# A selective-scan stage re-laid: 32 channels by 4 states per instruction, operands spread by DMA, decays in PSUM

## The chip, the cores and the metric

One core of one Trainium2 chip runs the whole program. The metric is device time in microseconds (us): the median of three runs, with one further execution taken by the profiler.

## What is computed

Two layers, each a Mamba block on a sequence of 2304 tokens (four images of 24 x 24, pixel-shuffled) and then a mixture of experts. The change touches only the Mamba block, cut here to what matters:

```
u = silu(conv4(in_proj(x)) + conv_b)             # 128 channels
dt, B, C = split(x_proj(u))                      # B and C: 16 states each
dt = softplus(dt_proj(dt) + dt_b)                # 128 channels
for each step:
    h[d, n] = exp(dt[d] * A[d, n]) * h[d, n] + dt[d] * u[d] * B[n]
    y[d]    = sum_n h[d, n] * C[n]
out = out_proj((y + u * D) * silu(z))
```

Everything is in float32. Softplus is computed as relu(x) + ln(1 + e) plus what the rounding of 1 + e lost, with e = exp(-|x|).

## The kernel before

`mamba` works through 24 tiles of T = 384 steps. Each engine has its own program, written out by hand, and the engines meet only at semaphores; each engine takes its instructions in the order written. An inner loop over n goes through the 16 states. Channels lie on the 128 partitions and one instruction takes one state, 128 x 384:

- ScalarE `decay` (L487) writes exp(dt * A[n]) into `da`, a ring of eight buffers in SBUF (`NDA` = 8), so it can be eight states ahead of the scan.
- TensorE `spread_b` (L373) spreads row n of B over all partitions by a bf16 matmul with a selector; B is held as a sum of three bf16 parts, which VectorE splits off (`split_one` L560, `split_two` L568) with two ScalarE copies.
- VectorE `times_b` (L577) multiplies w = dt * u with the spread B in place in PSUM, and `scan` (L586) runs the recurrence h = da * h + dbu along the 384 steps.
- GpSimd `times_c` (L657) multiplies h with C spread over the partitions. C gets there by DMA: its rows are stored (`c_rows`, L701) and read back by four broadcasting transfers (`crep`, L706).
- TensorE `sum_y` (L382) adds the 16 products up in PSUM by matmuls with the identity; `skip` (L378) starts the sum with u * D. The sum has two PSUM banks in turn.

For the next tiles, between those: TensorE `u_in` (L345), `z_in` (L355), `project_bc` (L362), `project_dt` (L366), and `project_out` (L388) for the tile before; ScalarE `silu_u` (L457), `silu_z` (L463) and six softplus steps (L226 to L244) with three table loads a tile (L536, L538, L542); GpSimd four additions and products that end softplus and form w (L248 to L262); VectorE `gate` (L593, y times silu(z)) and `residual` (L598, which adds `project_out`'s result to X). `project_out` and `z_in` share one PSUM bank, `zb_ps`: `z_in` of the next tile waits for `residual`.

## Time and profile before

| | |
|---|---|
| median of 3 runs | 2034.57 us (2032.19 to 2036.46) |
| the profiled execution | 2032.55 us, span of its instructions 2030.8 us |
| first to last scan, layer 0 | 46.96 to 622.3 us |
| VectorE busy | 1483.5 us (73% of the span) |
| TensorE matmul busy | 1643.1 us (81%) |
| GpSimd busy | 1216.9 us (60%) |
| ScalarE busy | 981.5 us (48%) |

Busy shares are means over stages with different limits. Two stretches of the span, one for each layer, are the Mamba blocks; the rest (norms, routing, experts, combining) is not touched. In a timeline row an instruction can start before the one ahead of it is over, so start-to-start distances are what adds up.

### The profile page before, as it was taken

Reading aid. Unit: us, or ns where it says so; the run is one execution under the profiler, and the core shown is the slowest. Engines: PE = TensorE matmul, PEld = TensorE weight load, DVE = VectorE, ACT = ScalarE, POOL = GpSimd, SP = SyncE. Lnnn points to the kernel's source line nnn. Section 1 sums busy time; section 2 is a strip of 40 time slices with the busy share of each in tenths; the row PEclk is TensorE's granted clock in tenths of the full one; section 3 lists DMA queues with packets and bytes.
Section 4 is the critical chain, followed back from the end, with each engine's and each line's share of the span. In section 5 each row is a group of like instructions: output and inputs, shape, how many; then the busy total and the mean of one; then the engine's idle time right before and its main releaser. Section 6 shows DMA issues by size and latency. Waiting matters only on the chain. (4 is left out here: it accounts for less than half of the span.)

```text
span 2030.8 us, 31247 instructions
## 1 busy us (share of the span) xinstructions
PE 1643.1 (81%) x7952; PEld 1124.3 (55%) x7953; DVE 1483.5 (73%) x2441; ACT 981.5 (48%) x1739; POOL 1216.9 (60%) x1409
## 2 busy tenths in 40 slices
PE   6888888888878399999946888888888874699994
PEld 4444444444435299999934444444444433599992
DVE  4999999999995522222246999999999986444443
ACT  6777677766763011111137777667766643011111
POOL 1888888888882135454305888888888860355440
PEclk8999999999999699999977999999999997799996
DMA  4344433333336301011033334433333326011114
GB/s 157 128 141 142 143 134 125 125 125 125 125 125 259 135 32 38 34 39 34 29 118 125 126 134 141 144 143 126 125 125 125 125 82 276 27 52 46 46 44 148
DMA packets 60049, 227.06 MB, mean 112 GB/s; under 512 B 8448, under 2 KB 23680, under 8 KB 56576
## 3 DMA queue, kind: packets, MB, share of 16 engines
q1 hardware_dynamic: 51744, 203.93, 28.1%
q0 software_dynamic: 8256, 22.56, 3.4%
q8 instruction: 21, 0.34, 0.1%
q14 instruction: 28, 0.23, 0.0%
HBM read 206.92 MB, written 19.53 MB: 112 GB/s over the span
## 5 line engine op out<-in xcount | busy, mean ns | idle before, releaser
L657 POOL TENSOR_TENSOR L_hc<-L_h,L_crep 128x384 f32<-128x384 f32 x768 | 775.2, 1018 | 211.1 <-DVE L_h L586 211.1
L382 PE MATMUL ps<-L_hc,ident 128*128 128x384 f32 x1536 | 622.4, 487 | 0.9 <-POOL L_hc L657 0.8
L577 DVE TENSOR_TENSOR ps<-L_w,ps 128x384 f32<-128x384 f32 x768 | 414.9, 540 | 20.4 <-PE ps L373 10.4
L487 ACT ACTIVATE L_da<-L_dt,L_negA 128x384 f32<-128x384 f32 x768 | 414.9, 604 | 15.6 <-DVE L_h L586 15.0
L373 PE MATMUL ps<-L_parts,sel 96*128 96x384 bf16 x768 | 256.3, 335 | 183.6 <-DVE L_h L586 177.3
L586 DVE TENSOR_TENSOR_SCAN L_h<-L_da,L_carry,ps 128x384 f32<-128x384 f32 x384 | 384.6, 1002 | 0.0
L586 DVE TENSOR_TENSOR_SCAN L_h<-L_da,L_h,ps 128x384 f32<-128x384 f32 x384 | 383.6, 999 | 0.0
L373 PEld LDWEIGHTS ps<-L_parts,sel 96*128 96x128 bf16 x768 | 73.4, 96 | 501.7 <-DVE L_h L586 494.3
L382 PEld LDWEIGHTS ps<-L_hc,ident 128*128 128x128 f32 x1536 | 270.9, 193 | 39.4 <-issue 6.2
L1114 DVE COPY Xn<-L_w 128x2048 f32 x86 | 107.8, 1256 | 117.6 <-PE ps L1064 108.8
L1097 ACT ACTIVATE L0e_hT<-ps 128x512 f32<-128x512 f32 x86 | 51.4, 597 | 267.4 <-PE ps L1064 267.4
L1064 PE MATMUL ps<-L0e_xT,Xn 128*128 128x128 f32 x1376 | 159.7, 277 | 2.8 <-DVE Xn L1114 2.8
L1064 PEld LDWEIGHTS ps<-L0e_xT,Xn 128*128 128x128 f32 x1376 | 159.4, 194 | 4.3 <-issue 3.2
L1064 PE MATMUL ps<-L1e_xT,Xn 128*128 128x128 f32 x1376 | 158.9, 277 | 2.6 <-DVE Xn L1114 2.6
L1064 PEld LDWEIGHTS ps<-L1e_xT,Xn 128*128 128x128 f32 x1376 | 158.2, 194 | 4.5 <-issue 2.9
L1079 PE MATMUL ps<-L_w,L0e_hT 128*128 x688 | 152.2, 379 | 0.9 <-ACT L0e_hT L1097 0.9
L1079 PEld LDWEIGHTS ps<-L_w,L0e_hT 128*128 128x128 f32 x688 | 129.0, 190 | 17.7 <-issue 1.1
L1097 ACT ACTIVATE L1e_gl<-ps 128x512 f32<-128x512 f32 x43 | 25.7, 598 | 217.6 <-PE ps L1064 217.6
L345 PEld LDWEIGHTS ps<-Xn,L_fold 128*128 128x128 f32 x480 | 89.5, 199 | 38.8 <-ACT L_sp_r L229 3.5
L345 PE MATMUL ps<-Xn,L_fold 128*128 (+1 forms) x480 | 105.4, 338 | 2.3 <-ACT L_sp_r L229 2.3
L1002 POOL TENSOR_TENSOR L0e_give_done<-ones 128x1 f32<-128x1 f32 x44 | 8.5, 194 | 164.0 <-DVE L0e_yt L1136 162.2
L1136 DVE COPY L0e_yt<-ps 128x512 f32<-128x512 f32 (+1 forms) x22 | 14.9, 680 | 123.2 <-PE ps L1079 123.2
(270 smaller groups left out, 2052.0 us busy)
## 6 DMA issues: line engine op xcount, KB each, us to landing
L_crep<-c_rows SPq DMA_DIRECT2D x192, 768.0 KB, 7.6
L_w<-in_up SPq DMA_DIRECT2D x16, 1024.0 KB, 11.9
L_w<-in_down SPq DMA_DIRECT2D x8, 1024.0 KB, 26.9
tok_rows<-Xn SPq DMA_DIRECT2D x6, 768.0 KB, 13.1
L0s_got<-results SPq DMA_DIRECT2D x18, 256.0 KB, 2.8
L1s_got<-results SPq DMA_DIRECT2D x18, 256.0 KB, 3.3
L_w<-in_down SPq DMA_DIRECT2D x8, 512.0 KB, 21.3
X<-in_x SPq DMA_DIRECT2D x4, 576.0 KB, 7.7
```

What stands on the lines that cost most here:

```text
L345: mm = nc.tensor.matmul(ua_ps[:, j * (T // 2):(j + 1) * (T // 2)], fold[:, g, :], column(t, img, back), start=(k in (0, 2)), stop=(k in (1 ...
L373: nc.tensor.matmul(b_ps(n), m["sel"][:, n, :], parts[0:BC, r, :], start=True, stop=True).then_inc(sem["b"], 1)
L382: nc.tensor.matmul(y_ps[r], ident[:], hc[:, n % NHC, :], start=False, stop=(n == N - 1)).then_inc(sem["y"], 1)
L487: nc.scalar.activation(da[:, n % NDA, :], dt[:, r, :], ACT.Exp, scale=negA[:, 0, n:n + 1]).then_inc(sem["da"], 1)
L577: nc.vector.tensor_tensor(b_ps(n), w[:, r, :], b_ps(n), ALU.mult).then_inc(sem["dbu"], 1)
L586: nc.vector.tensor_tensor_scan(h[:, n, :], da[:, n % NDA, :], b_ps(n), first, ALU.mult, ALU.add).then_inc(sem["scan"], 1)
L657: nc.gpsimd.tensor_tensor(hc[:, n % NHC, :], h[:, n, :], crep[:, r, n, :], ALU.mult).then_inc(sem["hc"], 1)
L1064: mm = nc.tensor.matmul(ps[:, h * NBH + b, (f % BF) * TS:(f % BF + 1) * TS], w1_t[:, h, i, f * P:(f + 1) * P], xT[:, r, i, h, :], start=(i ...
L1079: mm = nc.tensor.matmul(ps[:, 7, h * D:(h + 1) * D], hT[:, r, h, f, :], w2[:, bass.ds(e[h], 1), f, :].rearrange("p e d -> p (e d)"), start ...
L1097: nc.scalar.activation(dst, ps[:, h * NBH + b, :], ACT.Silu if gated else ACT.Gelu).then_inc(sem["act"], 1)
L1114: nc.vector.tensor_copy(w1_t[:, h].rearrange("p i f -> p (i f)"), w1[:, bass.ds(e, 1)].rearrange("p e i f -> p (e i f)")).then_inc(sem["st ...
L1136: nc.vector.tensor_copy(yt[:, r, 0:n, :].rearrange("p h d -> p (h d)"), ps[:, 7, 0:n * D]).then_inc(sem["yev"], 1)
```

## The change

The state is laid out otherwise. Partition 32 n + d now holds channel d of a group of 32 channels and the n-th quarter of the states, so one instruction takes 32 channels x 4 states; column c = 4 k + g is state k of each quarter and channel group g. There are still 16 columns of 128 x 384 a tile.

- dt and w must now stand in every quarter. TensorE adds the three parts of softplus in PSUM (`add_relu`, `add_log`), of which GpSimd forms only the lost rounding (`lost`); ScalarE copies dt out (`take_dt`), VectorE forms w (`times_u`). SP stores both (`dw_rows`, 384 KB) and reads them back into `dwq` by four transfers of 384 KB, one for each quarter of the partitions, and then C and the last four states' B from `cb_rows` into `cbq` by four of 240 KB. In place of that, the spread of C to 128 partitions goes (3 MB a tile).
- B of 12 states is spread by three float32 matmuls a tile; the three-part bf16 split goes. One instruction multiplies two columns: six a tile on VectorE, into SBUF, two on GpSimd (`times_b`).
- Decays are written to PSUM, three banks in turn (`DA_RING` = 3) in place of eight buffers in SBUF.
- `times_c` takes two columns at a time (eight a tile in place of sixteen).
- `sum_y` takes four columns at a time: four float32 matmuls with a 128 x 32 matrix, each into its own 32 partitions of the sum. The sum has one PSUM bank; `skip` waits for the gate of the tile before.
- ScalarE computes Ln with the table set that has Exp too, so two table loads a tile are left. Softplus of tile t + 2 is worked on in tile t.

```diff
-NDA, NHC = 8, 8
-NBP = 4
-LEAD, LAG = 3, 5
-A0, A1 = 4, 11
-D_GATE, D_SPLIT, D_RES = 5, 2, 8
-P0, P1 = 5, 7
-CN = 4
+Q = 4
+QW = P // Q
+QR = Q + 1
+DA_RING = 3
...
+        def da(r, c):
+            return bank((r * N + c) % DA_RING)
+        def b_ps(r, k):
+            return bank(3 + (r + k) % 2)
+        y_ps, ua_ps, zb_ps = bank(5), bank(6), bank(7)
...
             def u_in(t, img, which):
                 if 0 in which:
-                    wait(pe, sem["relu"], t)
+                    wait(pe, sem["w"], t)
+                    wait(pe, sem["dt_out"], t)
...
+            def add_relu(t):
+                pe.wait_ge(sem["relu"], t + 1)
+                nc.tensor.matmul(ua_ps, ident[:], sp["r"][:], start=True, stop=False)
+            def add_log(t):
+                pe.wait_ge(sem["l"], t + 1)
+                nc.tensor.matmul(ua_ps, ident[:], sp["l"][:], start=False, stop=False)
+                pe.wait_ge(sem["lost"], t + 1)
+                nc.tensor.matmul(ua_ps, ident[:], sp["a"][:], start=False, stop=True).then_inc(sem["dt"], 1)
+            def spread_b(t, r, k):
+                wait(pe, sem["dbu"], 6 * t + 2 * k - 2)
+                nc.tensor.matmul(b_ps(r, k), w_b[:, k, :], u[:, r, :], start=True, stop=True).then_inc(sem["b"], 1)
             def skip(t, r):
-                wait(pe, sem["yz"], t - 1)
-                nc.tensor.matmul(y_ps[r], diagD[:], u[:, r, :], start=True, stop=False)
-            def sum_y(t, r, n):
-                pe.wait_ge(sem["hc"], t * N + n + 1)
-                nc.tensor.matmul(y_ps[r], ident[:], hc[:, n % NHC, :], start=False, stop=(n == N - 1)
-                                 ).then_inc(sem["y"], 1)
+                wait(pe, sem["yz"], t)
+                nc.tensor.matmul(y_ps, diagD[:], u[:, r, :], start=True, stop=False)
+            def sum_y(t, r, k):
+                pe.wait_ge(sem["hc"], 8 * t + 2 * k + 2)
+                for g in range(Q):
+                    mm = nc.tensor.matmul(y_ps[g * QW:(g + 1) * QW, :], same[:, 0:QW], hc[:, (k % 2) * Q + g, :],
+                                          start=False, stop=(k == Q - 1))
+                mm.then_inc(sem["y"], 1)
...
+                if more:
+                    add_relu(t + 1)
+                    add_log(t + 1)
+                if not first:
+                    sum_y(t - 1, 1 - r, Q - 1)
+                spread_b(t, r, 2)
+                if more == 2:
+                    u_in(t + 2, img2, (0, 1))
+                if not first:
                     if more:
-                        if n == 0:
-                            project_bc(t + 1, 1 - r)
-                        if n == 1:
-                            project_dt(t + 1, 1 - r)
-                    if more == 2 and 4 <= n <= 6:
-                        u_in(t + 2, img2, ((0, 1), (2, 3), (4,))[n - 4])
-                    if n == 6 and not first:
-                        if more:
-                            pe.wait_ge(sem["r1"], t + 2)
-                        project_out(t - 1)
-                    if n == 8 and more:
-                        z_in(t + 1, img1)
+                        pe.wait_ge(sem["bc_out"], t + 2)
+                    else:
+                        pe.wait_ge(sem["zs"], t + 1)
+                    project_out(t - 1)
+                skip(t, r)
+                if more == 2:
+                    u_in(t + 2, img2, (2, 3, 4))
+                sum_y(t, r, 0)
+                if more:
+                    spread_b(t + 1, 1 - r, 0)
+                    wait(pe, sem["bc_out"], t + 2)
+                    wait(pe, sem["res"], t)
+                    z_in(t + 1, img1)
+                sum_y(t, r, 1)
+                if more:
+                    spread_b(t + 1, 1 - r, 1)
+                if more == 2:
+                    project_dt(t + 2, r)
+                    pe.wait_ge(sem["zs"], t + 2)
+                    project_bc(t + 2, r)
+                sum_y(t, r, 2)
...
+            def take_dt(t, before):
+                act.wait_ge(sem["dt"], t + 1)
+                for s, count in before:
+                    wait(act, s, count)
+                nc.scalar.activation(dw[:, 0, :], ua_ps, ACT.Identity, bias=ln_one[:, 1:2]).then_inc(sem["dt_out"], 1)
...
+            def decay(t, r, p, c):
+                at = r * N + c
+                if c == 0:
+                    act.wait_ge(s_dw[r], 64 * (p + 1))
+                if at < DA_RING:
+                    wait(act, sem["scan"], 2 * N * p + (-1, 0, -2)[at])
+                else:
+                    act.wait_ge(sem["scan"], 2 * N * p + at - DA_RING + 1)
+                nc.scalar.activation(da(r, c), dwq[:, r, c % Q, 0, :], ACT.Exp, scale=negA[:, 0, c:c + 1]
                                      ).then_inc(sem["da"], 1)
...
+            def tile(t, r, p, more):
+                for c in range(N):
+                    decay(t, r, p, c)
+                    if c == 1 and more:
+                        take_dt(t + 1, [(s_dw_row[r], 16 * (p + 1))])
+                    if more != 2:
+                        if c == 9 and more:
+                            nc.scalar.preload_act_table_set(SILU)
+                            silu_z(t + 1, 1 - r)
+                            nc.scalar.preload_act_table_set(EXP_LN)
                         continue
-                    if n == A0:
-                        b_high(t + 1)
-                    if n == A0 + 1:
-                        dt_head(t + 1, 1 - r)
-                        steps(t + 1, r)[2]()
-                    if n == A0 + 2:
-                        b_mid(t + 1)
-                        steps(t + 1, r)[3]()
-                    if n == A0 + 3:
-                        steps(t + 1, r)[4]()
-                    if n == A1:
-                        nc.scalar.preload_act_table_set(LN)
-                        steps(t + 1, r)[5]()
+                    if c == 9:
                         nc.scalar.preload_act_table_set(SILU)
-                        if more == 2:
-                            silu_u(t + 2, r)
+                        silu_u(t + 2, r)
                         silu_z(t + 1, 1 - r)
                         nc.scalar.preload_act_table_set(EXP_LN)
+                    if c == 12:
+                        dt_head(t + 2)
+                    if c == 13:
+                        steps(t + 2)[2]()
+                        take_bc(t + 2, [(s_cb_row[1 - r], 16 * (p + 1 + r))])
+                    if c == 14:
+                        steps(t + 2)[3]()
+                    if c == 15:
+                        steps(t + 2)[4]()
+                        steps(t + 2)[5]()
...
+            def times_b(t, r, p, k, i):
+                dve.wait_ge(sem["b"], 3 * t + k + 1)
+                if k == 0 and i == 0:
+                    dve.wait_ge(s_dw[r], 64 * (p + 1))
+                q = 2 * k + i
+                if q >= 3:
+                    dve.wait_ge(sem["scan"], t * N + 2 * q - 4)
+                else:
+                    wait(dve, sem["scan"], (t - 1) * N + 2 * q + 8)
+                at = 2 * (q % 3)
+                nc.vector.tensor_tensor(dbu[:, at:at + 2, :], dwq[:, r, 2 * i:2 * i + 2, 1, :], spread(b_ps(r, k)),
+                                        ALU.mult).then_inc(sem["dbu"], 1)
...
+                nc.vector.tensor_tensor_scan(h[:, c, :], da(t % 2 if isinstance(t, int) else int(slot is None), c),
+                                             dbu[:, c % 6, :] if k < Q - 1 else dbp[:, g, :], first, ALU.mult, ALU.add
                                              ).then_inc(sem["scan"], 1)
...
+            def times_u(t, r, before):
+                dve.wait_ge(sem["dt_out"], t + 1)
+                for s, count in before:
+                    wait(dve, s, count)
+                nc.vector.scalar_tensor_tensor(out=dw[:, 1, :], in0=ua_ps, scalar=ln_one[:, 1:2], in1=u[:, r, :],
+                                               op0=ALU.add, op1=ALU.mult).then_inc(sem["w"], 1)
...
+                for j in range(N // 2):
+                    k, i = (j + 1) // 2, (j + 1) % 2
+                    if k < Q - 1:
+                        times_b(t, r, p, k, i)
+                    elif j == N // 2 - 1 and not last:
+                        times_b(t + 1, 1 - r, p + r, 0, 0)
+                    scan(t, 2 * j, slot)
+                    scan(t, 2 * j + 1, slot)
+                    if j == 1 and not last:
+                        times_u(t + 1, 1 - r, [(s_dw_row[r], 16 * (p + 1))])
+                    if not (isinstance(t, int) and t == 0):
+                        if j == 2:
+                            gate(t - 1, 1 - r)
+                        if j == 3:
+                            residual(t - 1)
...
+            def lost(t):
+                pool.wait_ge(sem["g"], t + 1)
+                nc.gpsimd.tensor_tensor(sp["a"][:], sp["e"][:], sp["g"][:], ALU.subtract).then_inc(sem["lost"], 1)
+            def times_c(t, r, p, j):
+                k = j // 2
+                if j == 0:
+                    pool.wait_ge(s_cb[r], 64 * (p + 1))
+                if j % 2 == 0:
+                    wait(pool, sem["y"], Q * t + k - 1)
+                pool.wait_ge(sem["scan"], t * N + 2 * j + 2)
+                nc.gpsimd.tensor_tensor(hc[:, 2 * j % 8:2 * j % 8 + 2, :], h[:, 2 * j:2 * j + 2, :],
+                                        spread(cbq[:, r, k, :]), ALU.mult).then_inc(sem["hc"], 1)
+            def times_b(t, r, p, i):
+                if i == 0:
+                    pool.wait_ge(s_cb[r], 64 * (p + 1))
+                    pool.wait_ge(s_dw[r], 64 * (p + 1))
+                    wait(pool, sem["scan"], t * N)
+                nc.gpsimd.tensor_tensor(dbp[:, 2 * i:2 * i + 2, :], dwq[:, r, 2 * i:2 * i + 2, 1, :],
+                                        spread(cbq[:, r, Q, :]), ALU.mult).then_inc(sem["dbu_p"], 1)
...
+                if not last:
+                    lost(t + 1)
+                for j in range(N // 2):
+                    times_c(t, r, p, j)
+                    if j in (1, 2):
+                        times_b(t, r, p, j - 1)
...
+            def send(t, r, p):
+                gone, there = count(64 * p), count(16 * (p + 1))
+                bc_out, dt_out, w = count(t + 1), count(t + 1), count(t + 1)
+                decayed, driven, mixed, driven_p = count((t - 1) * N), count((t - 1) * 6), count((t - 1) * 8), count((t - 1) * 2)
+                sp_.wait_ge(sem["bc_out"], bc_out)
+                wait(sp_, s_cb[r], gone)
+                sp_.dma_start(cb_rows[r].rearrange("n (k t) -> (n k) t", t=T), bc[0:Q * QR, :]).then_inc(s_cb_row[r], 16)
+                sp_.wait_ge(sem["dt_out"], dt_out)
+                sp_.wait_ge(sem["w"], w)
+                wait(sp_, s_dw[r], gone)
+                sp_.dma_start(dw_rows[r], dw[:].rearrange("p x t -> p (x t)")).then_inc(s_dw_row[r], 16)
+                sp_.wait_ge(s_dw_row[r], there)
+                wait(sp_, sem["da"], decayed)
+                wait(sp_, sem["dbu"], driven)
+                wait(sp_, sem["dbu_p"], driven_p)
+                for n in range(Q):
+                    sp_.dma_start(dwq[n * QW:(n + 1) * QW, r].rearrange("p g x t -> p g (x t)"),
+                                  dw_rows[r].rearrange("(g d) t -> d g t", g=Q)).then_inc(s_dw[r], 16)
+                sp_.wait_ge(s_cb_row[r], there)
+                wait(sp_, sem["hc"], mixed)
+                for n in range(Q):
+                    sp_.dma_start(cbq[n * QW:(n + 1) * QW, r].rearrange("p k t -> p (k t)"),
+                                  cb_rows[r, n].unsqueeze(0).to_broadcast([QW, QR * T])).then_inc(s_cb[r], 16)
```

## Rows read from the trace of the kernel before

**Rows 1.** The page: engines' busy time, and the granted TensorE clock in 40 slices.
```profile
PE 1643.1 (81%) x7952; PEld 1124.3 (55%) x7953; DVE 1483.5 (73%) x2441; ACT 981.5 (48%) x1739; POOL 1216.9 (60%) x1409
...
PEclk8999999999999699999977999999999997799996
```

**Rows 2.** Window of one tile: length, busy by engine, clock, DMA share, GB/s.
```profile
199.70:223.70 24.00, 19.92 (x75) 10.90 (x75) 24.00 (x38) 17.11 (x30) 19.95 (x21) 1.00 0.39 133
```

**Rows 3.** Timeline, VectorE: first and last scans of layer 0 (start, length, instruction).
```profile
46.96 1.01 DVE L586 TENSOR_TENSOR_SCAN L_h<-L_da,L_carry,ps 128x384 f32<-128x384 f32 x1
...
620.40 1.90 DVE L586 TENSOR_TENSOR_SCAN L_h<-L_da,L_h,ps 128x384 f32<-128x384 f32 x2
```

**Rows 4.** Timeline, VectorE: one state in the steady part.
```profile
207.30 0.54 DVE L577 TENSOR_TENSOR ps<-L_w,ps 128x384 f32<-128x384 f32 x1
...
207.75 1.00 DVE L586 TENSOR_TENSOR_SCAN L_h<-L_da,L_carry,ps 128x384 f32<-128x384 f32 x1
...
208.67 0.54 DVE L577 TENSOR_TENSOR ps<-L_w,ps 128x384 f32<-128x384 f32 x1
```

**Rows 5.** Groups by line and form: busy us, mean ns | idle before, releaser.
```profile
L560 DVE SCALAR_TENSOR_TENSOR L_r<-L_hi,mask,ps 96x384 f32<-96x384 bf16 x48 | 28.1, 585 | 8.8 <-ACT L_hi L469 8.8
L593 DVE TENSOR_TENSOR L_yz<-L_zs,ps 128x384 f32<-128x384 f32 x48 | 25.2, 525 | 4.4 <-PE ps L382 4.4
L598 DVE TENSOR_TENSOR X<-X,ps 128x192 f32 x40 | 12.9, 324 | 0.0
L153 DVE TENSOR_TENSOR Xn<-X,ps 128x768 f32<-128x768 f32 x12 | 11.4, 954 | 17.0 <-PE ps L129 17.0
...
L487 ACT ACTIVATE L_da<-L_dt,L_negA 128x384 f32<-128x384 f32 x768 | 414.9, 604 | 15.6 <-DVE L_h L586 15.0
L542 ACT ACT_TABLE_LOAD x46 | 59.0, 1283 | 0.8
L463 ACT ACTIVATE L_zs<-ps 128x384 f32<-128x384 f32 x48 | 25.3, 526 | 119.8 <-PE ps L355 119.8
...
L657 POOL TENSOR_TENSOR L_hc<-L_h,L_crep 128x384 f32<-128x384 f32 x768 | 775.2, 1018 | 211.1 <-DVE L_h L586 211.1
L248 POOL TENSOR_TENSOR L_tok<-L_tok 128x1 f32<-128x1 f32 x2 | 0.4, 195 | 0.0
```

**Rows 6.** Timeline: GpSimd behind a scan; nine decays of ScalarE back to back.
```profile
621.54 1.95 POOL L657 TENSOR_TENSOR L_hc<-L_h,L_crep 128x384 f32<-128x384 f32 x2 [0.37 <-DVE L_h L586]
...
207.75 4.66 ACT L487 ACTIVATE L_da<-L_dt,L_negA 128x384 f32<-128x384 f32 x9
```

**Rows 7.** Waits of ScalarE, 150 to 640 us: us in total, times, longest.
```profile
ACT L_zs L463 <- PE ps L355: 50.4, 19, 3.1
```

**Rows 8.** Timeline, TensorE back to back: two halves of one sum, then four of u_in.
```profile
222.58 0.81 PE L382 MATMUL ps<-L_hc,ident 128*128 128x384 f32 x2
...
223.23 0.81 PE L345 MATMUL ps<-Xn,L_fold 128*128 x4
```

**Rows 9.** Layer 0's beginning: windows as in group 2, and a float32 matmul.
```profile
42.00:48.00 6.00, 1.59 (x2) 0.40 (x2) 2.31 (x5) 5.96 (x10) 3.52 (x7) 0.61 1.01 367
48.00:54.00 6.00, 3.95 (x10) 2.12 (x10) 6.00 (x10) 4.72 (x12) 4.00 (x4) 0.50 0.14 34
...
48.31 1.49 PE L366 MATMUL ps<-L_u,L_w_dt 128*128 128x384 f32 x2
```

**Rows 10.** DMA: KB each and median us to landing; one tile's GB/s in 40 slices of 218 to 232 us; its issues.
```profile
L_crep<-c_rows SPq DMA_DIRECT2D x192, 768.0 KB, 7.6
...
out<-X SPq DMA_DIRECT2D x3, 768.0 KB, 4.8
...
c_rows<-L_r SPq DMA_DIRECT2D x48, 24.0 KB, 1.5
...
GB/s 0 0 0 0 18 53 0 0 0 176 105 193 316 386 334 281 263 369 421 351 281 351 316 334 351 369 386 281 334 316 492 334 527 334 509 211 70 0 0 0
...
220.38 1.96 SPq L706 DMA_DIRECT2D L_crep<-c_rows  x4
```

375 lines of the change are left out of this document (136 added, 239 removed).

## The prediction

> **What bounds the kernel now.** Three views, from far to near. The page says that no engine is full over the whole span [rows 1], so the stage has to be read by itself. The window of one tile does that: VectorE is busy in all of its 24.00 us, TensorE in 19.9, GpSimd in 20.0, ScalarE in 17.1, the DMA engines in 39% [rows 2]. A layer's scans run from 46.96 to 622.3 us, 575.3 us for 24 tiles or 23.97 us a tile [rows 3]. The timeline gives the price of VectorE's work: a product starts 0.45 us before its scan, and the next product 0.92 us after the scan's start [rows 4]. Durations shown are some 0.08 us longer than these distances, and I take that off the others [rows 5]: 0.50 for a split, 0.44 for the gate, 0.24 for the residual. 16 x 1.37 + 2 x 0.50 + 0.44 + 0.24 = 23.60 us; the other 0.37 are the carry's copy and small waits. So VectorE bounds the stage, and the others hide behind it, because they may run ahead: ScalarE by eight decays. It uses that. It stood 50.4 us in 19 tiles, 2.7 us a tile, waiting for z out of TensorE before `silu_z` [rows 7], and no scan was late for it.
>
> **What the change takes off VectorE.** A product of 2 x 384, one operand in PSUM and spread, one in SBUF, is what L153 is: 954 ns, so 0.87 from start to start [rows 5]. Six of them are 5.22 us in place of 16 x 0.45 = 7.2. Scans stay 16 x 0.92 = 14.72: no row has a scan with its decay in PSUM, but both forms read one operand from each memory. Two splits go, `times_u` comes (0.50, as L560). With gate and residual the tile is 21.12 us: 2.85 us less than 23.97. With nothing else, 48 tiles would give 137 us; that is the most that it can bring.
>
> **What it costs: the decay ring is now three.** ScalarE can write decay c only when scan c - 3 is over, so whatever keeps ScalarE for more than about two scans stops VectorE. I put VectorE's tile in order from its start, without waits: product 0, scans 0 and 1 at 0.87 and 1.79, product, scans 2 and 3 at 3.58 and 4.50, `times_u` 5.42, product 5.92, scans 4 and 5 at 6.79 and 7.71, gate 8.63, product 9.07, scans 6 and 7 at 9.94 and 10.86, residual 11.78, product 12.02, scans 8 to 13 at 12.89 to 17.49, product 18.41, scans 14 and 15 at 19.28 and 20.20. Two places stop it.
>
> *First stall, at `take_dt`.* It stands behind decay 1 and ahead of decay 2, and waits for dt of the next tile, thus for `lost`, which GpSimd issues only after the last `times_c` of the tile before. The last scan ends 0.08 us into the tile; GpSimd starts 0.14 behind it [rows 6]. A product of 2 x 384 there: 195 ns for one element, 1018 for 384 [rows 5], hence 1.84 us for 768 (bounds 1.8 and two times 1.0). `lost` 1.0 more: 3.0 us. TensorE's last add 0.81 [rows 8]: 3.9. `take_dt` some 0.5, then decay 2 takes 0.60 [rows 5] and is there at 5.0, and the scan wanted it at 3.58. Stall 1.45 us (1.0 if the decay into PSUM takes 0.5 and GpSimd is as quick as it can be, 1.9 if GpSimd takes 2.0 and starts late). Decays into PSUM have no row; back-to-back ones into SBUF start 0.52 apart [rows 6], 0.60 is alone, and I keep 0.60.
>
> *Second stall, at `silu_z`.* z of the next tile now stands behind the gate. The sum has one bank, so `skip` waits for the gate, and on TensorE everything is behind `project_out`, which waits for it too. From the gate's end at 8.63 + 1.45 + 0.53 = 10.6, plus 0.2 to get there, TensorE has in a row: `project_out`, `skip`, three of `u_in`, `sum_y` of four columns, `spread_b`, `z_in`. A float32 matmul of 384 columns takes 0.65 from start to start and ends 0.16 later; one of 192, 0.33 [rows 8]. That is 0.65 + 0.65 + 0.98 + 4 x 0.65 + 0.65 + 0.65 = 6.2, so z is there at 17.1. `silu_z` 0.53 and a table load 1.28 [rows 5], then decay 10 0.60: 19.6. Scan 10 is due at 14.73 + 1.45 = 16.2. Stall 3.4 us. If z cost no wait, the block of two table loads and two silus behind decay 9 (12.5 + 0.52 + 1.28 + 1.03 + 1.28 + 0.60 = 17.2) would still stall it by 1.0: that is the lower bound. After that, scans 11 to 15 ask for one decay per 0.92 us, and ScalarE's 16 decays at 0.52 and its other work at some 0.5 each keep up. Before, the same two waits had five more buffers to hide in.
>
> The tile: 21.12 + 1.45 + 3.4 = 25.97 us, 2.0 more than before.
>
> **What else is added, hidden or not.** GpSimd has 8 + 2 products of 1.84 and `lost`, 19.4 us in 26: hidden. Its B products are done by about 14 us and scan 12 wants them at 21. TensorE: 25 float32 matmuls of 384 columns at 0.65 (16 for the sums, 3 for B, 3 for dt, `skip`, `project_bc`, `project_dt`), and 2.9 for `u_in`, `z_in` and `project_out`: 19.2 us, enough room, but in pieces. The DMA way from `times_u` (done at 7.4): storing 384 KB lies between 24 KB at 1.5 us and 768 KB at 4.8 us, I take 3.1; then the spread. Four transfers of 768 KB took from 220.38 to about 230.9 us, 1.5 until they flow and 9 for 3.1 MB [rows 10]. 1.57 MB: 6.1 us, so dwq is there at 16.7; the next tile's first product wants it at 18.41 + 4.85 = 23.3. `cbq` (0.98 MB) comes at 19.6, and GpSimd wants it at about 29. SP's eight issues at 0.5 us hide, and the transfers they are queued behind are these. If the stalls were not there, dwq would come at 15.3 for 18.4: 3 us to spare.
>
> The row has transfers to all 128 partitions; here each goes to 32. The Trainium skill (SBUF — State Buffer, Door 1, the DMA port swizzle) says that partitions 0 to 31 reach only 8 of the 16 ports, which speaks against the change. By it the spreads would run at half the rate: dwq at 21.3 in place of 16.7, still ahead of 23.3 and the sum unchanged, but 1.5 us late if the stalls are not there.
>
> Once a layer: the way to the first scan gets the store and the spread, less one table load, +6 us; the tail a GpSimd product of two columns and a longer sum, +3. Tile 0 has neither gate nor wait for `lost`: 22.1. Tile 22 has no `u_in`: 25.0. Tile 23 has no block on ScalarE: 21.1.
>
> **The sum.** A layer: 21 x 25.97 + 22.1 + 25.0 + 21.1 = 613.6, +38.3 against 575.3; with +9 it is +47.3. Two layers: +95 us. The profiled execution took 2032.55 us (span 2030.8 and 1.75 around it), 2.0 below the median and inside the runs' 4.3: 2032.55 + 95 = 2127 us. I take 0.2% (4 us) as what a measurement can tell from no change.
>
> **Rivals.**
>
> *The four strips of `sum_y` overlap* (chance 0.20). No row here has a matmul of 32 columns. The rows' price is one after another. A float32 matmul is two instructions of 0.33 us; if those of different strips run beside each other and those of one strip don't, four take five slots, 1.63 in place of 2.6. z comes 1.0 earlier, the tile is 25.0, and the sum 2 x (21 x 25.0 + 67.3 + 9 - 575.3), with tile 22 shorter too: 2083. The Trainium skill states such a rule (TensorE: Matmul & The Clock Gate, Part 3, packing small matmuls): outputs placed at PSUM partitions 32j land in separate column groups and run at once. Fully overlapped (0.65) it would be 24.1 a tile and 2045.
>
> *The clock falls* (0.19). Now TensorE works nearly without a gap, and the granted clock is 1.00 in the stage [rows 2]. At a layer's start, where it was busy 1.6 us of 6, the clock went to 0.61 and stood at 0.50 in the next 6 us with 3.95 us busy, and a float32 matmul pair took 1.49 in place of 0.81 [rows 9]. That is 1.2 GHz for 2.4. After, TensorE waits some 1.5 us for `lost`, 2.5 for the gate and 3.5 for the fourth pair of products, every tile. If a quarter of the 6.2 + 0.65 us in the two chains were run at the low clock, it is +1.7 us a tile: 2198. At worst, half the chain: 2270. For it: the pieces. Against it: the total stays above half.
>
> *The stalls don't form, and it gets faster* (0.24). One mechanism: z arrives before ScalarE asks for it, at 14.8 in place of 17.1, because the chain behind the gate is shorter than my sum of starts. Then the second stall is the block's own 1.0 and the tile 23.5: 21 x 23.54 + 22.1 + 23.5 + 21.1 + 9 = 570.0, 5.3 less than 575.3, twice: 2022 us. It decides from 2.3 us less in that chain; a tile breaks even at 23.8, that is with 2.6 us of stalls in place of 4.85. Without any stall but that 1.0 the kernel would go to some 1960.
>
> *The DMA way sets the tile* (0.05). If store and spread took 16 us from `times_u` in place of 9.3, every tile would wait: 2150 and up.
>
> **How the numbers follow.** My forecast, both stalls with sums in a row and the clock kept, 2100 to 2150, has 0.32; the others as given. The likeliest is 2127. The range runs from 2020, the faster rival's sum with half of its chance below, to 2200, the clock's middle with half of its chance above; the likeliest's own range is 2100 to 2150. Of the faster rival's 0.24 about 0.03 fall within 0.2% of no change, and 0.01 of full overlap's: faster 0.21, within 0.04, slower 0.75.
>
> **What would show it.** Right: products of 2 x 384 on VectorE near 954 ns and scans near 1000; VectorE idle 4 to 5 us a tile, before scan 2 and scan 10, released by ScalarE's decays; ScalarE waiting at `take_dt` for TensorE and at `silu_z` for `z_in`; scans of a layer 600 to 620 us from first to last. Wrong: VectorE without idle time before scan 10 (z came early), stalls at the first product released by the DMA, matmuls of 1.49 with a clock under 0.9, or GpSimd products of two columns far from 1.84 us. I would be wrong most easily in the length of TensorE's chain and in what it is granted.

## The result, and the profile after the change

The changed kernel takes 2184.05 us (median of 4 runs, 2183.41 to 2184.64), the kernel before 2033.38: the ratio is 1.0742 (95% interval 1.0725 to 1.0759), 151 us slower. The forecast was 2127.

The page of the changed kernel: busy time, and the granted TensorE clock in 40 slices [rows 1].

```profile
PE 1570.9 (72%) x7776; PEld 1034.5 (47%) x7777; DVE 1358.4 (62%) x1913; ACT 934.6 (43%) x1695; POOL 1171.5 (54%) x980
...
PEclk9777777777776789999978777777777777599996
```

VectorE has 125 us less to do than before, and the kernel is 151 us longer. No other engine has filled up: all four have a smaller share than before. Only waits can do that. The clock row says something more: 9 in the stage before, 7 after.

The first scans and the last group of scans of layer 0, timeline of VectorE [rows 3]:

```profile
55.61 1.92 DVE L588 TENSOR_TENSOR_SCAN L_h<-ps,L_carry,L_dbu 128x384 f32<-128x384 f32 x2
...
694.06 3.72 DVE L588 TENSOR_TENSOR_SCAN L_h<-ps,L_h,L_dbp 128x384 f32<-128x384 f32 x4
```

From 55.61 to 697.78 are 642.2 us, 26.76 a tile, where 575.3 stood before. The layer starts its scans 8.65 us later. Twice (66.9 + 8.65) is 151.1 us: the whole difference, within 1 us, is in this stage of the two layers.

The groups by line (busy us, mean ns of one | idle before, releaser) show the price of each instruction:

```profile
L671 POOL TENSOR_TENSOR L_hc<-L_h,L_cbq 128x768 f32<-128x768 f32 x384 | 697.2, 1817 | 397.2 <-DVE L_h L588 375.3
L490 ACT ACTIVATE ps<-L_dwq,L_negA 128x384 f32<-128x384 f32 x768 | 429.4, 576 | 247.2 <-DVE L_h L588 236.1
L588 DVE TENSOR_TENSOR_SCAN L_h<-ps,L_h,L_dbu 128x384 f32<-128x384 f32 x288 | 276.3, 1001 | 139.1 <-ACT ps L490 139.1
L588 DVE TENSOR_TENSOR_SCAN L_h<-ps,L_carry,L_dbu 128x384 f32<-128x384 f32 x288 | 276.6, 1002 | 113.6 <-ACT ps L490 113.6
L575 DVE TENSOR_TENSOR L_dbu<-L_dwq,ps 128x768 f32<-128x768 f32 x288 | 270.3, 939 | 26.2 <-DMA L_dwq<-dw_rows 13.2
```

The scans wait 252.7 us for a decay of ScalarE. The DMA row is 13.2 us in the whole run, the two layer starts: the spreads are hidden everywhere else.

Where the scans wait, in a pair of tiles (timeline, VectorE, only rows with idle time ahead of them):

```profile
303.27 1.93 DVE L588 TENSOR_TENSOR_SCAN L_h<-ps,L_h,L_dbu 128x384 f32<-128x384 f32 x2 [2.32 <-ACT ps L490]
318.48 1.92 DVE L588 TENSOR_TENSOR_SCAN L_h<-ps,L_h,L_dbu 128x384 f32<-128x384 f32 x2 [3.99 <-ACT ps L490]
325.76 0.95 DVE L575 TENSOR_TENSOR L_dbu<-L_dwq,ps 128x768 f32<-128x768 f32 x1 [0.65 <-DVE L_carry L650]
330.20 1.93 DVE L588 TENSOR_TENSOR_SCAN L_h<-ps,L_carry,L_dbu 128x384 f32<-128x384 f32 x2 [0.81 <-ACT ps L490]
345.63 1.92 DVE L588 TENSOR_TENSOR_SCAN L_h<-ps,L_carry,L_dbu 128x384 f32<-128x384 f32 x2 [4.20 <-ACT ps L490]
```

There are two stalls a tile, before scan 2 (0.81 and 2.32 in turn) and before scan 10 (4.20 and 3.99). A pair of tiles in the steady part takes 54.6 us, and 11.3 of them are these four. Tiles 1 to 22 of each layer have both, 44 tiles in all; tile 0 has 1.27 and 1.21 us before scans 10 and 13, tile 23 none. The 0.65 us behind the copy of the carry (the last state, handed on from pair to pair) come once in two tiles.

The rows behind them, one tile, all engines (start, length):

```profile
215.73 1.81 POOL L671 TENSOR_TENSOR L_hc<-L_h,L_cbq 128x768 f32<-128x768 f32 x1 [0.86 <-DVE L_h L588]
217.50 1.00 POOL L662 TENSOR_TENSOR L_sp_a<-L_sp_e,L_sp_g 128x384 f32<-128x384 f32 x1
218.54 0.91 PE L350 MATMUL ps<-L_sp_a,ident 128*128 128x384 f32 x2 [1.79 <-POOL L_sp_a L662]
219.58 0.58 ACT L471 ACTIVATE L_dw<-ps,L_ln_one 128x384 f32<-128x384 f32 x1 [3.31 <-PE ps L350]
220.95 1.92 DVE L588 TENSOR_TENSOR_SCAN L_h<-ps,L_carry,L_dbu 128x384 f32<-128x384 f32 x2 [0.81 <-ACT ps L490]
...
226.00 0.53 DVE L603 TENSOR_TENSOR L_yz<-L_zs,ps 128x384 f32<-128x384 f32 x1
226.67 1.62 PE L370 MATMUL ps<-L_yz,L_wp 128*128 128x192 f32 x4 [1.67 <-DVE L_yz L603]
228.09 1.48 PE L358 MATMUL ps<-L_u,L_diagD 128*128 128x384 f32 x2
229.36 1.96 PE L323 MATMUL ps<-Xn,L_fold 128*128 x6
231.25 0.85 PE L363 MATMUL ps<-L_hc,same 128*32 128x384 f32 x8
232.03 0.91 PE L354 MATMUL ps<-L_u,L_wp 128*128 128x384 f32 x2
232.78 0.81 PE L330 MATMUL ps<-Xn,L_wp 128*128 x4
233.63 0.54 ACT L458 ACTIVATE L_zs<-ps 128x384 f32<-128x384 f32 x1 [1.65 <-PE ps L330]
234.19 1.28 ACT L543 ACT_TABLE_LOAD   x1
235.49 1.59 ACT L490 ACTIVATE ps<-L_dwq,L_negA 128x384 f32<-128x384 f32 x3
236.39 1.93 DVE L588 TENSOR_TENSOR_SCAN L_h<-ps,L_carry,L_dbu 128x384 f32<-128x384 f32 x2 [4.21 <-ACT ps L490]
```

Both chains of the forecast are there link by link: last product, `lost`, TensorE's add, `take_dt`, decay 2; gate, `project_out`, `skip`, `u_in`, `sum_y`, `spread_b`, `z_in`, `silu_z`, table load, decay 10. Two lengths are not those of the forecast. `skip` takes 1.48 in place of 0.81, and `project_out` (four matmuls of 192 columns) 1.62: half speed. And the eight 32-column matmuls of `sum_y` take 0.85 together, in place of 2.6 + 0.16.

The clock in windows of 2 us of the same tile (length, busy of PE, PEld, DVE, ACT, POOL, clock, DMA share, GB/s):

```profile
226.00:228.00 2.00, 1.33 (x4) 1.36 (x5) 2.00 (x4) 0.58 (x1) 2.00 (x2) 0.50 0.62 143
228.00:230.00 2.00, 2.00 (x5) 1.39 (x5) 2.00 (x4) 1.63 (x2) 2.00 (x2) 0.50 1.08 229
230.00:232.00 2.00, 2.00 (x13) 1.14 (x12) 2.00 (x3) 0.87 (x2) 1.85 (x2) 0.75 1.03 226
232.00:234.00 2.00, 2.00 (x18) 1.16 (x14) 0.17 (x1) 0.37 (x1) 1.70 (x1) 1.00 1.11 220
```

The chain behind the gate starts at 1.2 GHz and comes back to 2.4 towards the end of `u_in`, at 231.0. What came before it: TensorE waited 2.67 us for w (`times_u`) up to 223.75 and 1.67 us for the gate up to 226.67. These two things, a chain in order and a clock that the chain's own waits bring down, are what the experiments separate.

### The profile page after: what moved, and what is told of

It reads as the page before. It is cut to its first block and busy times, and to the rows that moved or that the text cites. A ratio compares the mean times of both kernels' runs of the same rounds, so it can differ in the third digit from the quotient of the medians.

```text
span 2182.9 us, 28861 instructions
## 1 busy us (share of the span) xinstructions
PE 1570.9 (72%) x7776; PEld 1034.5 (47%) x7777; DVE 1358.4 (62%) x1913; ACT 934.6 (43%) x1695; POOL 1171.5 (54%) x980
## 5 line engine op out<-in xcount | busy, mean ns | idle before, releaser
L671 POOL TENSOR_TENSOR L_hc<-L_h,L_cbq 128x768 f32<-128x768 f32 x384 | 697.2, 1817 | 397.2 <-DVE L_h L588 375.3
L490 ACT ACTIVATE ps<-L_dwq,L_negA 128x384 f32<-128x384 f32 x768 | 429.4, 576 | 247.2 <-DVE L_h L588 236.1
L588 DVE TENSOR_TENSOR_SCAN L_h<-ps,L_h,L_dbu 128x384 f32<-128x384 f32 x288 | 276.3, 1001 | 139.1 <-ACT ps L490 139.1
L588 DVE TENSOR_TENSOR_SCAN L_h<-ps,L_carry,L_dbu 128x384 f32<-128x384 f32 x288 | 276.6, 1002 | 113.6 <-ACT ps L490 113.6
L363 PE MATMUL ps<-L_hc,same 128*32 128x384 f32 x1536 | 189.8, 571 | 183.6 <-POOL L_hc L671 183.5
L575 DVE TENSOR_TENSOR L_dbu<-L_dwq,ps 128x768 f32<-128x768 f32 x288 | 270.3, 939 | 26.2 <-DMA L_dwq<-dw_rows 13.2
L679 POOL TENSOR_TENSOR L_dbp<-L_dwq,L_cbq 128x768 f32<-128x768 f32 x96 | 174.2, 1814 | 0.0
L354 PE MATMUL ps<-L_u,L_wp 128*128 128x384 f32 x288 | 150.4, 608 | 11.3 <-DVE L_dbu L575 11.3
L370 PE MATMUL ps<-L_yz,L_wp 128*128 128x192 f32 x192 | 77.7, 557 | 85.8 <-DVE L_yz L603 85.8
L350 PE MATMUL ps<-L_sp_a,ident 128*128 128x384 f32 x96 | 60.9, 726 | 85.0 <-POOL L_sp_a L662 85.0
```

The costliest lines, as they stand in the source:

```text
L354: nc.tensor.matmul(b_ps(r, k), w_b[:, k, :], u[:, r, :], start=True, stop=True).then_inc(sem["b"], 1)
L363: mm = nc.tensor.matmul(y_ps[g * QW:(g + 1) * QW, :], same[:, 0:QW], hc[:, (k % 2) * Q + g, :], start=False, stop=(k == Q - 1))
L370: mm = nc.tensor.matmul(zb_ps[:, 0:T // 2], w_out[:, j, :], js(yz[:])[:, j, :], start=(j == 0), stop=(j == 1))
L490: nc.scalar.activation(da(r, c), dwq[:, r, c % Q, 0, :], ACT.Exp, scale=negA[:, 0, c:c + 1]).then_inc(sem["da"], 1)
L575: nc.vector.tensor_tensor(dbu[:, at:at + 2, :], dwq[:, r, 2 * i:2 * i + 2, 1, :], spread(b_ps(r, k)), ALU.mult).then_inc(sem["dbu"], 1)
L588: nc.vector.tensor_tensor_scan(h[:, c, :], da(t % 2 if isinstance(t, int) else int(slot is None), c), dbu[:, c % 6, :] if k < Q - 1 else d ...
```

## The experiments

Each kernel is the changed kernel with the edit shown, and is compared with the kernel before (2033.0 to 2033.3 us in these runs).

**1. The clock alone.** Dummy matmuls (identity by identity, into columns or a bank that nothing reads then) are put where TensorE waits: before the wait for `lost`, before `u_in`, before `project_out`, before `sum_y(t, r, 2)`. The first two stand behind one more wait, for `bc_out`, which frees their bank.

```
+            def warm_z(n):
+                for _ in range(n):
+                    nc.tensor.matmul(zb_ps[:, 0:P], ident[:], ident[:], start=True, stop=True)
...
+                    warm_z(4)
                 pe.wait_ge(sem["lost"], t + 1)
...
+                    warm_z(8)
...
+                        warm_z(4)
                     project_out(t - 1)
...
+                    warm_y(8)
                 sum_y(t, r, 2)
```

> The changed kernel with small matmuls of the identity with itself added on TensorE in its four idle places of a tile (before the wait for lost, before u_in, before project_out, before sum_y of the third group); their results go to columns and to a bank that nobody reads then. Nothing else is changed. If the low clock is what took the time beyond my forecast, the granted clock goes from 0.75 in the stage to over 0.95, z comes some 2.5 us earlier after the gate, the idle time before scan 10 falls from 4.2 to under 2 us, and the kernel goes from 2184 to 2050 to 2080. If the order alone stops VectorE and the clock only goes along with it, the time stays within 10 us of 2184.

Measured: 2088.86 us, ratio 1.0274 (1.0255 to 1.0292), 9 us above the expected range. The clock in the stage (150 to 600 us) is 0.96 instead of 0.75. One stall before scan 10, and the next one before scan 2:

```profile
320.43 1.92 DVE L605 TENSOR_TENSOR_SCAN L_h<-ps,L_carry,L_dbu 128x384 f32<-128x384 f32 x2 [2.02 <-POOL L_hc L688]
...
331.96 1.92 DVE L605 TENSOR_TENSOR_SCAN L_h<-ps,L_h,L_dbu 128x384 f32<-128x384 f32 x2 [1.58 <-ACT ps L507]
```

The stall before scan 10 is 2.0 in every steady tile (4.1 without the dummies), and the one before scan 2 is mostly 0.81 and 1.58 in turn (0.81 and 2.32). GpSimd is named as releaser, but the product that scan 10 waits for is one of the tile before, long over; what ended the stall is decay 10, started at 319.53. So the low clock is worth 95 us, nearly two thirds of the loss, less than the theory's middle of 119: 2.1 us in 44 tiles (92) before scan 10, and some 0.3 (11) before scan 2. The other 55 us are there at the high clock. What the dummies themselves may add to a wait is in that.

**2 to 4. The order alone.** The gate one product earlier (after scan 3, residual after scan 5); `take_dt` after decay 3; both.

```
-                        if j == 2:
+                        if j == 1:
                             gate(t - 1, 1 - r)
-                        if j == 3:
+                        if j == 2:
                             residual(t - 1)
```
```
-                    if c == 1 and more:
+                    if c == 3 and more:
                         take_dt(t + 1, [(s_dw_row[r], 16 * (p + 1))])
```

> The changed kernel with gate one pair of scans earlier (behind times_u, j = 1 in place of 2) and residual too (j = 2 in place of 3). If z standing behind the gate is what stops scan 10, z comes about 3 us earlier and the time falls by 22 tiles x 2 layers x 2.5 to 3 us, to 2050 to 2075. If scan 10 is held by the length of ScalarE's block of silus and table loads or by the ring of three alone, it falls by less than 20 us.

> The changed kernel with take_dt behind decay 3 in place of decay 1. If the wait for lost before decay 2 is a stall of its own, the idle time before scan 2 (0.8 us in the tile I read) goes, and the time falls by some 40 to 60 us, to 2125 to 2145. If the time that it gives back is waited off again at scan 10, it falls by less than 10 us.

> Both: gate and residual one pair earlier, take_dt behind decay 3. If the two stalls add up, the time is 2184 less the sum of what the two do alone, 2000 to 2030, a little under the kernel before (2033). If they share one wait, it is near the better of the two.

Measured: gate 2107.14 (ratio 1.0372, 1.0354 to 1.0391), 77 us less, where 109 or more were expected; `take_dt` 2071.02 (1.0195, 1.0177 to 1.0214), 113 less, where 40 to 60 were expected; both 2030.45 (0.999, 0.998 to 1.0), 154 less, at the upper end of what was expected. The two gains add up to 190, not 154: part of what `take_dt` gives alone is a shorter wait for z, and with the gate early nobody waits for z.

Why `take_dt` gave twice its own stall, two scans 10 of that kernel say:

```profile
312.78 1.93 DVE L588 TENSOR_TENSOR_SCAN L_h<-ps,L_carry,L_dbu 128x384 f32<-128x384 f32 x2 [2.08 <-POOL L_hc L671]
...
337.29 1.92 DVE L588 TENSOR_TENSOR_SCAN L_h<-ps,L_h,L_dbu 128x384 f32<-128x384 f32 x2 [3.42 <-ACT ps L490]
```

In the first tile the gate ended at 305.06 and `z_in` at 310.01, 4.95 us; in the second at 328.22 and 334.52, 6.30 us. Over all tiles of four kernels the stall before scan 10 follows that length one for one:

| kernel | gate's end to `z_in`'s end | stall before scan 10 |
|---|---|---|
| clock held (1) | 4.89 | 2.0 |
| `take_dt` later (3), five sorts of tile | 4.95, 6.30, 6.43, 7.21, 7.89 | 2.1, 3.4, 3.6, 4.4, 5.0 |
| changed kernel, in turn | 6.87, 7.06 | 4.0, 4.2 |
| `lost` earlier (9), in turn | 6.53, 7.26 | 3.7, 4.4 |

The stall is the chain less 2.9 us. In this kernel TensorE's chain ran at the high clock in 9 of 18 tiles, and it is 5.96 us on average in place of 6.96. So `take_dt` gave 1.57 us a tile (the mean of 0.81 and 2.32) plus 1.0: times 44 that is 113, as measured. What TensorE did before the chain has changed too: in those 18 tiles it waited 0.44 us on average for w ahead of `u_in`, where the changed kernel has 1.81 (2.67 and 0.94 in turn). That this wait is what brought the clock back in half of the tiles is likely and not shown by itself.

Why the gate gave less than expected: one pair of tiles of that kernel, rows with idle time.

```profile
477.20 1.93 DVE L588 TENSOR_TENSOR_SCAN L_h<-ps,L_carry,L_dbu 128x384 f32<-128x384 f32 x2 [1.55 <-ACT ps L490]
481.21 1.02 DVE L588 TENSOR_TENSOR_SCAN L_h<-ps,L_carry,L_dbp 128x384 f32<-128x384 f32 x1 [1.17 <-ACT ps L490]
490.75 1.92 DVE L588 TENSOR_TENSOR_SCAN L_h<-ps,L_h,L_dbu 128x384 f32<-128x384 f32 x2 [2.32 <-ACT ps L490]
503.66 1.93 DVE L588 TENSOR_TENSOR_SCAN L_h<-ps,L_h,L_dbu 128x384 f32<-128x384 f32 x2 [1.45 <-ACT ps L490]
```

z is in time now. Before scan 10 there is a floor of 1.45 to 1.55 us, ScalarE's own block of two table loads and two silus, where the forecast had 1.0. The first stall is still there (1.66 on average in 18 tiles, 1.57 before), and a third one appears before scan 13: up to 1.2 us, 0.45 on average. That is 4.1 - 1.5 - 0.45 - 0.1, some 2.0 us a tile or 90 us in 44 tiles; measured were 77.

**5. Three PSUM banks, or the order?** The ring of decays gets eight buffers in SBUF, as before the change. First alone, then with both moves, and with the dummy matmuls too.

```
-DA_RING = 3
+DA_RING = 8
...
-            return bank((r * N + c) % DA_RING)
+            return das[:, (r * N + c) % DA_RING, :]
...
```

> The decays go into eight buffers of 384 columns in SBUF in place of three PSUM banks; nothing else changes, the lines stand in the order of the changed kernel. Theory A (the order of the instructions sets the stalls): before scan 10 VectorE waits for decay 10, and decay 10 stands behind silu_z on ScalarE, which waits for z_in on TensorE; a deeper ring lets no decay past it. The stall before scan 10 stays at 2 to 4 us, the one before scan 2 too (take_dt stands after decay 1), and the time stays at 2165 to 2190. Rival B (three banks are the fault: the ring lets ScalarE lead by three states where the kernel before let it lead by eight): the stalls shrink by the two table loads that the ring can't cover, 1.5 us or more a tile, and the time falls by 70 us or more, to 2115 or below. Rival C (scans that read both streams from SBUF beside GpSimd's products get slower): scans above 1.05 us and a time over 2200.

> Both moves of the order (gate after scan 3 and residual after scan 5, take_dt after decay 3) and the ring of eight decays in SBUF. With both moves alone the trace had 1.45 to 1.56 us before scan 10 with ScalarE at work all the time (two table loads and two silus, 3.6 us, where three banks hold decays for 3 scans), and 0.9 to 1.0 us before scan 13, behind the first two steps of the softplus. Theory A: now that TensorE's z_in comes in time, the ring is what is left; both stalls go, some 2.3 us a tile over 48 tiles is 110 us, and the time is 1915 to 1960. Rival B (the ring never matters): within 15 us of the 2030 of both moves alone.

> All of it: both moves, ring of eight, idle matmuls. Theory A: with the ring of eight ScalarE reaches silu_u and silu_z earlier and may wait for TensorE again, so the clock can be worth 5 to 25 us here: 1900 to 1950. Rival B (the idle matmuls only stand in the way once nothing waits for TensorE): slower than both moves with the ring of eight by 5 us or more.

Measured: 2488.19 (ratio 1.2244, 1.2224 to 1.2265), 2445.20 (1.2031, 1.2011 to 1.2051), 2444.21 (1.2024, 1.2004 to 1.2044). None of the three is in a range that theory A or rival B gave; the dummy matmuls change nothing (1 us). The price of a scan was the surprise. Groups of 150 to 600 us, with both moves:

```profile
L589 DVE TENSOR_TENSOR_SCAN L_h<-L_das,L_h,L_dbu 128x384 f32<-128x384 f32 x84 | 140.5, 1717 | 0.0
L589 DVE TENSOR_TENSOR_SCAN L_h<-L_das,L_carry,L_dbu 128x384 f32<-128x384 f32 x84 | 134.0, 1640 | 0.0
L576 DVE TENSOR_TENSOR L_dbu<-L_dwq,ps 128x768 f32<-128x768 f32 x85 | 79.1, 931 | 4.6 <-DVE L_carry L651 4.6
...
L672 POOL TENSOR_TENSOR L_hc<-L_h,L_cbq 128x768 f32<-128x768 f32 x112 | 220.6, 1970 | 138.2 <-DVE L_h L589 138.2
L680 POOL TENSOR_TENSOR L_dbp<-L_dwq,L_cbq 128x768 f32<-128x768 f32 x28 | 69.6, 2485 | 0.0
```

A scan whose decay and drive both lie in SBUF takes 1640 to 1717 ns, not 1001; the product with one operand in PSUM keeps its price. GpSimd's products grow too, those with C from 1817 to 1970 ns, those with B from 1814 to 2485. VectorE's idle time before the scans is gone (0.0), as the theory of the ring said, and the kernel is 412 us slower than the one before the change all the same, 261 slower than the changed one. Rival C was right. That it takes GpSimd at work, and not the two streams alone, shows in the kernel with the ring of eight and nothing else, where GpSimd stood idle from 689.48 to 691.80:

```profile
689.80 1.93 DVE L589 TENSOR_TENSOR_SCAN L_h<-L_das,L_h,L_dbu 128x384 f32<-128x384 f32 x2 [1.37 <-ACT L_das L491]
```

Both streams in SBUF, and the two scans take their usual 1.93 us. For the ring's own worth these runs say nothing; run 8 was made for that. They do show that the PSUM ring is no whim of the change: with the drive in SBUF and GpSimd at work beside the scans, the decay is better kept elsewhere.

**6. Does the clock cost anything by itself?** Both moves, three banks, and the dummy matmuls of run 1.

> Both moves of the order, three PSUM banks, and the idle matmuls of the first experiment, which keep TensorE's clock up. Theory A (the clock costs time only through the wait for z_in and for take_dt, and with both moves ScalarE no longer waits for z_in): granted clock above 0.9 and a time of 2005 to 2035, no better than both moves alone by more than 25 us. Rival B (the low clock costs its 95 us by itself, whatever the order): 1935 to 1950.

Measured: 2035.51 (ratio 1.0014, 1.0004 to 1.0024) with a clock of 0.97 in the stage, 5 us slower than both moves alone (clock 0.82 there). The waits of VectorE, 150 to 600 us (total, times, longest), of this kernel:

```profile
DVE L_h L605 <- ACT ps L507: 27.8, 19, 1.6
DVE X L625 <- PE ps L381: 12.3, 13, 1.9
```

and of both moves without the dummies:

```profile
DVE L_h L588 <- ACT ps L490: 36.3, 28, 1.6
...
DVE X L608 <- PE ps L370: 0.3, 1, 0.3
```

The stall before scan 10 is 1.45 or 1.55 in either. The high clock took 8.5 us of other stalls away, and the dummies, which `project_out` is queued behind, made the residual wait 12.3. So the clock's 95 us of run 1 were the length of what ScalarE waited for, nearly all of it the one chain behind the gate. Once ScalarE no longer waits for it, those 95 us are not there to win. What the clock would give without the dummies' own cost is not measured.

**7. The third stall.** On top of both moves, `project_dt` and `project_bc` go ahead of `sum_y(t, r, 1)`.

```
+                if more == 2:
+                    project_dt(t + 2, r)
+                    pe.wait_ge(sem["zs"], t + 2)
+                    project_bc(t + 2, r)
                 sum_y(t, r, 1)
                 if more:
                     spread_b(t + 1, 1 - r, 1)
-                if more == 2:
-                    project_dt(t + 2, r)
-                    pe.wait_ge(sem["zs"], t + 2)
-                    project_bc(t + 2, r)
```

> Both moves of the order, and on TensorE project_dt and project_bc of tile t + 2 ahead of sum_y(t, r, 1) instead of behind it. With both moves alone ScalarE waited 1.51 us for project_dt at the head of the softplus (331.30 us), TensorE had stood 2.23 us before that in sum_y for GpSimd's product, and VectorE waited 1.03 us before scan 13. Theory (the order of TensorE's queue sets this stall too): the stall before scan 13 goes, up to 1.0 us a tile, 48 us in all, and the time is 1975 to 2005. Rival (another wait of the same size stands behind it: two steps of the softplus, 1.0 us, lie in the lead of three decays anyway): 2020 to 2035.

Measured: 2007.06 (ratio 0.9876, 0.9861 to 0.9891), 23 us less and 2 above the theory's range. VectorE's waits for decays, 150 to 600 us:

```profile
DVE L_h L588 <- ACT ps L490: 27.9, 19, 1.6
```

28 waits became 19, and all that are left are those before scan 10. The stall before scan 13 is gone, as the theory had it; it was only in about every second tile (8.4 us in 19 tiles, 21 us in 48), not in each.

**8. The ring's own worth, with one scan's contention.** On top of run 7, decay 9 gets a buffer in SBUF, the fifteen others stay in the three banks.

```
+OWN = 9
...
-            return bank((r * N + c) % DA_RING)
+            return das[:] if c == OWN else bank((c - (c > OWN)) % DA_RING)
...
```

> The kernel of the run before it, with decay 9 of each tile in a buffer of its own in SBUF, and the other fifteen in the three PSUM banks. ScalarE's block of table loads and silus then starts one scan earlier (0.9 to 1.8 us), and scan 9 alone reads both streams from SBUF. Theory A (three banks and the 3.7 us of the block make the 1.45 us before scan 10; a scan with both streams in SBUF costs up to 0.7 us more beside a GpSimd product): a gain of 0.5 to 1.2 us a tile, 20 to 55 us under the run before it. Rival B (the scan loses as much as the stall gives back, or the wait for z_in takes its place): within 15 us of it.

Measured: 1967.39 (ratio 0.9673, 0.966 to 0.9686), 40 us under run 7 and 66 under the kernel before. VectorE's waits for decays in 150 to 600 us:

```profile
DVE L_h L594 <- ACT ps L496: 0.9, 1, 0.9
```

and one scan 9 with what runs beside it on GpSimd:

```profile
312.82 1.82 POOL L677 TENSOR_TENSOR L_hc<-L_h,L_cbq 128x768 f32<-128x768 f32 x1
...
312.89 1.02 DVE L594 TENSOR_TENSOR_SCAN L_h<-ps,L_h,L_dbu 128x384 f32<-128x384 f32 x1
313.82 1.64 DVE L594 TENSOR_TENSOR_SCAN L_h<-L_das,L_h,L_dbu 128x384 f32<-128x384 f32 x1
```

The scan with its decay in PSUM runs its 1.02 us beside GpSimd's product. The next one, with both streams in SBUF, takes 1.64: it ends 0.82 us after the product's end at 314.64. In all 24 tiles of the layer scan 9 takes 1.10 to 2.23 us, and in each it ends 0.80 to 0.83 us after GpSimd's product. That one scan costs some 0.6 us and takes the 1.5 away. 0.9 a tile is 40 us in 44 tiles, as measured.

**9. The first stall's cause.** The changed kernel with `lost` one product earlier on GpSimd.

```
+            lost(1)
...
             def tile(t, r, p, last):
-                if not last:
-                    lost(t + 1)
                 for j in range(N // 2):
+                    if j == N // 2 - 1 and not last:
+                        lost(t + 2)
                     times_c(t, r, p, j)
...
```

> The changed kernel with one line moved on GpSimd: lost(t + 2) stands ahead of the last product with C of tile t, where the changed kernel has it behind; nothing else is moved. Theory (take_dt blocks the decays because lost stands behind a 1.82 us product): take_dt is free 1.8 us earlier, the stall before scan 2 (0.8 to 1.6 us a tile) goes, TensorE's idle gap gets shorter and its clock with it a little better: 2060 to 2145, as the move of take_dt gave 113 us. Rival (the block is elsewhere: with VectorE, which makes the last product late whatever stands in GpSimd's queue): within 20 us of 2184.

Measured: 2118.74 (ratio 1.0421, 1.0406 to 1.0437), 65 us less. One pair of tiles, rows with idle time:

```profile
382.37 1.93 DVE L588 TENSOR_TENSOR_SCAN L_h<-ps,L_carry,L_dbu 128x384 f32<-128x384 f32 x2 [4.42 <-ACT ps L490]
407.10 1.93 DVE L588 TENSOR_TENSOR_SCAN L_h<-ps,L_h,L_dbu 128x384 f32<-128x384 f32 x2 [3.65 <-ACT ps L490]
```

The stall before scan 2 is gone and the one before scan 10 has stayed, 4.03 on average where 4.1 stood. 1.57 x 44 is 69 us. It was GpSimd's order that held `take_dt`, and this run is also a test of the account of run 3: here the first stall goes without the chain getting shorter (6.9 us on average), and the gain is that stall alone. So it is not the first stall's going that brings the clock back. TensorE's wait ahead of `u_in`, 0.44 us on average in run 3, is 2.89 here.

**The layers side by side.** From first to last scan of layer 0, over 24. The work without waits is 21.12 by the forecast's sum and 0.33 for the wait of 0.65 us behind the carry's copy in every second tile: 21.45.

| kernel | us a tile | over 21.45 |
|---|---|---|
| before the change | 23.97 | other work |
| changed | 26.76 | 5.3 |
| gate early (2) | 24.96 | 3.5 |
| `lost` early (9) | 25.21 | 3.8 |
| clock held (1) | 24.63 | 3.2 |
| `take_dt` later (3) | 24.11 | 2.7 |
| both moves (4) | 23.37 | 1.9 |
| and `project_dt` early (7) | 22.92 | 1.5 |
| and decay 9 in SBUF (8) | 22.03 | 0.6, the slower scan |

## Why the forecast came out as it did

The direction and the mechanism hold, the size was short: +95 forecast, +151 measured.

*VectorE's work.* Right in its prices, with one term left out. Products 939 ns (954 taken), scans 1001, and the last row of the table, without the 0.6 of its slower scan, is within 0.1 us of 21.45. The change does what it says: the 2.5 us a tile that it takes off VectorE would be 121 us. But the forecast named 0.37 us a tile for "the carry's copy and small waits" in the kernel before and put nothing for them in the tile after. A steady tile without its two stalls is (54.6 - 11.3) / 2 = 21.65 us, 0.5 above the forecast's 21.12. (Two times 0.08 of this are the stalls' own: an instruction's row ends 0.08 us after the next one could have started, so the idle time in a row is that much shorter than the delay.)

*The first stall, 1.45 us.* Right in place, cause and mean: 0.81 and 2.32 in turn, 1.57. Run 9 shows the cause. The alternation I had not seen, and it has two halves. In one tile of two TensorE's add behind `lost` runs at the low clock:

```profile
245.70 1.65 PE L350 MATMUL ps<-L_sp_a,ident 128*128 128x384 f32 x2 [1.91 <-POOL L_sp_a L662]
```

where the tile above has 0.91. With the clock held, the stall of these tiles falls from 2.32 to 1.58. The rest, 1.58 against 0.81, is there at the high clock too: the short stall is that of the tiles that begin with the pause behind the carry's copy, in which GpSimd gets ahead.

*The second stall, 3.4 us.* Right in place, and the size is 4.1. It came out near by two errors of opposite sign, which is luck. The 6.2 us that TensorE has in a row behind the gate, with `sum_y` at 4 x 0.65, are too long at full clock: strips of 32 columns overlap fully (0.85 for all eight matmuls, 1.9 less), and from the gate's end to z the forecast has 6.5 us where run 1 measures 4.89. That was the first rival, and alone it makes the stall 2.0. But the clock fell in the stage to 0.75, and the chain became 6.87 to 7.06. That was the second rival, and run 1 prices it at 95 us. I had taken the two as alternatives, with a sum of their own each; both came together. The sum failed at "both stalls with sums in a row and the clock kept". The first rival's own sum is not met either: 2045 for full overlap, where run 1, with full overlap and the clock held, has 2089. (Its sum for five slots comes to 2084 with its own terms, not 2083.)

*The clock.* The argument against it was that TensorE's total stays above half. It did (304.7 us busy of 450 in the stage, 68%), and the clock fell all the same, to 0.75, where single waits of 1.7 to 3.6 us stand between short bursts. I had also priced it as a quarter of two chains at the low clock. In the changed kernel the first two links of the second chain are wholly slow and the third, `u_in`, mostly.

*The floor of 1.0 under the second stall.* It measures 1.45 to 1.55, and a stall before scan 13 that I had excluded (by saying that ScalarE's 16 decays and its other work keep up with scans 11 to 15) shows as soon as the others shrink: 1.2 us in some tiles, because `project_dt` stood behind a sum that waits for GpSimd (run 7).

*The faster rival.* It named the right lever, z earlier than ScalarE asks for it, and not its full price. With z in time and the first stall left (run 2), the kernel is at 2107, not 2022; it takes both moves to reach no change, and two more to win 66 us.

*DMA.* Hidden in the steady part, as forecast; only the layer's start pays, 8.65 us for 6. The 3 us of the tail are 1.3: the last gate starts 3.5 us behind the last scan, 2.2 before. For the spreads to 32 partitions the 2-us windows above show 220 to 229 GB/s with the DMA engines full, where the window 221 to 230 us of the kernel before has 326: 0.7 of that rate, where the forecast's sum went by the full rate and named half as what the page would give. By the table of the Trainium skill (SBUF — State Buffer, Door 1) transfers to 32 partitions had 189 GB/s in a measurement and can have 218, transfers to 128 had 328 and can have 436. The trace agrees with the 328 and lies 1 to 5% above the 218, so the port limit itself is borne out and only the ratio of one half is not. Nothing waited for the transfers in either case.

*The sum again with what the runs show.* Steady tile: 21.65 + 1.57 + 4.1 = 27.3, as measured, 1.3 more than the 25.97 forecast. Of these, 0.7 are the second stall, 0.1 the first, and 0.5 the small terms named above. 21 such tiles and two layers are 56 us, the size of the whole miss: some 29 for the second stall, 5 for the first, 22 for what was left out. The start (2.65 more a layer), the tail (1.7 less) and the odd tiles at both ends nearly cancel.
